# Half routers over more places, three of them in the next round, and pool's late operations behind its wait for an odd place

## What is computed

```python
x = x + conv(ln_c(x))            # ln_c(x) * sigmoid(conv3x3([max_c, mean_c]))
t = to_tokens(x)                 # (16, 112*112, 64)
n = ln_t(t)
probs = softmax(n @ router_w + router_b)
top_p, top_i = top_k(probs, 2);  top_p = top_p / sum(top_p)
t = t + sum_k top_p[k] * (n @ expert_w[top_i[k]] + expert_b[top_i[k]])
```

## Time and profile before

| | |
|---|---|
| median of 3 runs | 1394.77 us (1394.36 to 1395.02) |
| profiled execution, its own time | 1395.69 us |
| its span, first to last instruction | 1393.8 us |
| PE busy | 1294.6 us, 93% |
| DVE busy | 1240.0 us, 89% |
| POOL busy | 1066.0 us, 76% |
| ACT busy | 1052.0 us, 75% |

### The profile page before, as it was taken

How to read it: one execution, slowest core, us unless ns; L and a number is a source line. 1 busy time by engine, 2 the same in 40 slices (tenths; PEclk the granted TensorE clock), 3 DMA queues, 4 the chain that set the end, 5 groups by cost and what they waited for, 6 DMA issues and landing times.

```text
span 1393.8 us, 33104 instructions
## 1 busy us (share of the span) xinstructions
PE 1294.6 (93%) x11750; PEld 612.6 (44%) x11750; DVE 1240.0 (89%) x1527; ACT 1052.0 (75%) x3950; POOL 1066.0 (76%) x643
## 2 busy tenths in 40 slices
PE   8964999999999999999999999999999898889998
PEld 8853444444444444444444444444444332333332
DVE  6787799988999899998999799998999879998887
ACT  5677898888998889888898889888898533444442
POOL 5333787887888787877878878878878878789885
PEclk9955999999999999999999999999999999999999
DMA  6443466676666666576666666676666555657774
GB/s 224 120 123 89 132 207 206 174 224 199 198 187 213 194 204 199 173 226 199 199 200 199 199 200 200 187 217 192 207 203 175 163 166 162 175 167 205 205 204 144
DMA packets 85845, 259.97 MB, mean 187 GB/s; under 512 B 13744, under 2 KB 13744, under 8 KB 85680
## 3 DMA queue, kind: packets, MB, share of 16 engines
q1 hardware_dynamic: 85680, 257.85, 62.0%
HBM read 206.42 MB, written 51.38 MB: 185 GB/s over the span
## 4 chain that ended last, share of the span: by engine, by line
PE 56%; DVE 23%; issue 9%; POOL 2%; ACT 2%; DVEq 0%; POOLq 0%; ACTq 0%
PE moe L568 34%; DVE gx L714 13%; PE tm L493 8%; PE gb L514 8%; PE tm L507 2%; DVE ge L736 2%; DVE stats L691 2%; PE moe L562 2%; PE tm L553 2%; DVE ot L727 1%; DVE oh L749 1%; PE tm L592 1%; DVE u L799 1%; POOL dl L1265 1%; ACT sq L965 1%
## 5 line engine op out<-in xcount | busy, mean ns | idle before, releaser
L568 PE MATMUL moe<-gx,wc 128*64 128x448 f32 x3584 | 803.5, 551 | 0.0
L714 DVE TENSOR_TENSOR gx<-gb,xd 128x896 f32<-128x896 f32 x672 | 710.7, 1086 | 77.3 <-PE gb L514 72.9
L1205 POOL TENSOR_TENSOR gx<-gs,xd 128x896 f32<-128x896 f32 x224 | 492.8, 2200 | 228.0 <-ACT gs L1003 158.7
L965 ACT ACTIVATE sq<-xct 112x64 f32<-112x64 f32 x1400 | 338.4, 246 | 7.5 <-DVE early_s L701 2.1
L1003 ACT ACTIVATE gs<-gb 128x896 f32<-128x896 f32 x224 | 205.3, 916 | 176.4 <-PE gb L514 170.9
L568 PEld LDWEIGHTS moe<-gx,wc 128*64 128x64 f32 x3584 | 219.9, 136 | 201.6 <-issue 159.2
L965 ACT ACTIVATION_READ_ACCUMULATOR sq<-xct 112x1 f32 x1400 | 265.5, 190 | 0.0
L1222 POOL TENSOR_TENSOR tt<-xc,a1s 128x896 f32<-128x896 f32 x112 | 235.1, 2099 | 11.3 <-issue 9.7
L514 PE MATMUL gb<-s,cg 32*128 32x448 f16 x1792 | 175.6, 358 | 53.2 <-DVE gx L714 51.8
L514 PEld LDWEIGHTS gb<-s,cg 32*128 32x128 f16 x1792 | 48.0, 91 | 383.2 <-DVE gx L714 348.7
L493 PE MATMUL tm<-rhs,xa 64*112 64x74 f32 x2800 | 184.6, 272 | 10.6 <-ACT early_l L950 5.2
(11 more groups left out here) (94 smaller groups left out, 1090.0 us busy)
## 6 DMA issues: line engine op xcount, KB each, us to landing
xd<-in_x_dram SPq DMA_DIRECT2D x448, 224.0 KB, 4.0
xa<-in_x_dram SPq DMA_DIRECT2D x112, 448.0 KB, 4.5
xc<-in_x_dram SPq DMA_DIRECT2D x112, 448.0 KB, 4.8
out_dram<-ot SPq DMA_DIRECT2D x112, 448.0 KB, 3.6
gx<-in_const_g_dram SPq DMA_DIRECT2D x1, 384.0 KB, 5.5
cf<-in_const_f_dram SPq DMA_DIRECT2D x1, 333.5 KB, 3.1
cf<-in_L_ffn_expert_b_dram SPq DMA_DIRECT2D x12, 1.0 KB
gx<-in_L_ffn_expert_w_dram SPq DMA_DIRECT2D x1, 128.0 KB, 5.3
```

Source lines behind the costliest of these rows:

```text
L568: last = pe.matmul(moe[b * CH:(b + 1) * CH, c, 0:HALF], wc[:, k * CH:(k + 1) * CH], gx[:, u, b, :], start=False, stop=(k == KT - 1), skip_ ...
L714: dve.tensor_tensor(gx[:, i, :, :], gb[:, 2 * slot:2 * slot + 2, 0:HALF], xd[:, v % 2, :, c * HALF:(c + 1) * HALF], ALU.mult).then_inc(sca ...
L965: last = act.activation(sq[:, n, :], xct[:, step % 2, n, :], ACT.Square, accum_out=to[:, 1, lo + n:lo + n + 1])
L1205: pool.tensor_tensor(gx[:, ND + j, :, :], gs[:, j, :, :], xd[:, v % 2, :, j * HALF:(j + 1) * HALF], ALU.mult).then_inc(scaled_p, 1)
```

## The change

The half routers get other places. Half 0 has ten, 12 to 21: top; ge; key and key_max; oh1; dl; top2 and d; ge2; key2; key_max2; oh2. Half 1 has the first six of them at 22 to 27, and its last four operations go to three places of the next round: ge2 to place 0, key2 and key_max2 to place 4, oh2 to place 5. They count on a semaphore of their own, b_late, as B_LATE, and B_DVE has four operations less. ScalarE's part moves with them: `gates` of half 0 from step 8 to 9, the second widening of half 0 from 9 to 10, the first of half 1 from 11 to 12, `gates` of half 1 from 12 to step 0 of the next round, its second widening from 13 to step 2 of the next round. On pool the second, summed and scaled gates of half 0 move from steps 10, 11, 12 to 11, 12, 13; of half 1 first_gates moves from step 13 to step 0 of the next round, second_gates to step 2, summed and scaled gates to step 4, and all of these stand behind `router` and behind the wait for the odd place. The waits of pool for places are 1, 2, 3, 6, 7, 8 and 9 in rounds before 8 (26 is gone); in round 8 also 12 to 27, and in rounds 8 and 9 the late places 0, 4 and 5. rho has two buffers, since pool scales with the old one in step 4, after the next one has been written.

```diff
+B_LATE = ("ge2_1", "key2_1", "key_max2_1", "oh2_1")
 B_DVE = (tuple(n + "1" for n in ROOT) + ("r1", "av", "part_sum", "v2")
          + tuple(n + "2" for n in ROOT) + ("r2", "rho") + tuple(n + "_0" for n in HALF_ROUTER)
-         + tuple(n + "_1" for n in HALF_ROUTER))
+         + tuple(n + "_1" for n in HALF_ROUTER if n + "_1" not in B_LATE))
 B_POOL = ("lg_0", "bias_0", "lg_1", "bias_1", "m1_0", "m2_0", "qb_0", "qg_0", "m1_1", "m2_1", "qb_1",
           "qg_1")
 B_NORM = ("e1", "pool_max", "pool_mean", "am", "e2")
-B_ACT = ("sig", "wide_0", "g1_0", "g2_0", "qa_0", "wide2_0", "wide_1", "g1_1", "g2_1", "wide2_1", "qa_1")
+B_ACT = ("sig", "wide_0", "qa_0", "g1_0", "g2_0", "wide2_0", "wide_1", "g1_1", "g2_1", "qa_1", "wide2_1")
...
+        rhos = sb("rhos", [W, 2, 2 * H])
...
-        PLACE_END = {1: "t_a1", 2: "y_a1", 3: "r1", 6: "v2", 7: "t_a2", 8: "y_a2", 9: "rho",
-                     26: "key_max2_1"}
-
-        TAIL_END = {1: "t_a1", 2: "y_a1", 3: "r1", 6: "v2", 7: "t_a2", 8: "y_a2", 9: "rho"}
-        HALF_END = ("top", "ge", "key_max", "dl", "d", "ge2", "key_max2", "oh2")
-        for place in range(16):
-            TAIL_END[12 + place] = f"{HALF_END[place % 8]}_{place // 8}"
+        ROOT_END = {1: "t_a1", 2: "y_a1", 3: "r1", 6: "v2", 7: "t_a2", 8: "y_a2", 9: "rho"}
+        HALF_END = {12: "top_0", 13: "ge_0", 14: "key_max_0", 15: "oh1_0", 16: "dl_0", 17: "d_0", 18: "ge2_0",
+                    19: "key2_0", 20: "key_max2_0", 21: "oh2_0", 22: "top_1", 23: "ge_1", 24: "key_max_1",
+                    25: "oh1_1", 26: "dl_1", 27: "d_1"}
+        LATE_END = {0: "ge2_1", 4: "key_max2_1", 5: "oh2_1"}
 
         def vector_place(eng, r, place):
 
-            ends = TAIL_END if r == PAIRS else PLACE_END
-            if 1 <= r <= PAIRS and place in ends:
-                b_done(eng, r, B_DVE, ends[place])
+            if r <= PAIRS and place in ROOT_END:
+                b_done(eng, r, B_DVE, ROOT_END[place])
+            if r == PAIRS and place in HALF_END:
+                b_done(eng, r, B_DVE, HALF_END[place])
+            if PAIRS <= r <= PAIRS + 1 and place in LATE_END:
+                b_done(eng, r - 1, B_LATE, LATE_END[place])
...
                     own(r, f"top_{h}")
                     at_top(lg, top, rows).then_inc(b_dve, 1)
                 elif place == 2:
-                    largest_key(r, h, "", rows)
+                    tie_key(r, h, rows)
+                    first_of_ties(r, h, rows)
                 elif place == 3:
-                    first_expert(r, h)
+                    first_expert(r, h, rows)
                 elif place == 4:
-                    second_logit(r, h)
+                    logits_left(r, h, rows)
                 elif place == 5:
-                    own(r, f"top2_{h}")
-                    at_top(dl, top2, rows).then_inc(b_dve, 1)
+                    second_logit(r, h, rows)
                 elif place == 6:
-                    largest_key(r, h, "2", rows)
+                    second_at_top(r, h, rows, B_DVE)
+                elif place == 7:
+                    second_tie_key(r, h, rows, B_DVE)
+                elif place == 8:
+                    second_of_ties(r, h, rows, B_DVE)
                 else:
-                    second_expert(r, h)
+                    second_expert(r, h, rows, B_DVE)
+
+            def late_router(r, place):
+
+                if place == 0:
+                    second_at_top(r, 1, second, B_LATE)
+                elif place == 4:
+                    second_tie_key(r, 1, second, B_LATE)
+                    second_of_ties(r, 1, second, B_LATE)
+                elif place == 5:
+                    second_expert(r, 1, second, B_LATE)
...
-                if due(count := b_at(r, len(B_POOL), 0)):
+                if due(count := b_at(r - 1, len(B_POOL), 0)):
...
                     scale(r)
-                elif 12 <= place < 20:
+                elif 12 <= place < 22:
                     half_router(r, 0, place - 12)
-                elif place >= 20:
-                    half_router(r, 1, place - 20)
+                elif place >= 22:
+                    half_router(r, 1, place - 22)
...
+                    if tail:
+                        late_router(r - 1, 2 * step)
                     if Bp:
                         gate(r, step, False)
...
+                    if tail:
+                        late_router(r - 1, 2 * step + 1)
                     if Bp:
                         gate(r, step, True)
...
-                elif step == 8:
+                elif step == 9:
                     gates(r, 0)
-                elif step == 9:
+                elif step == 10:
                     widen(r, 0, "2")
-                elif step == 11:
+                elif step == 12:
                     widen(r, 1, "")
-                elif step == 12:
+
+            def late_router(r, step):
+
+                if step == 0:
                     gates(r, 1)
-                elif step == 13:
+                elif step == 2:
                     widen(r, 1, "2")
...
+                    if tail:
+                        late_router(r - 1, step)
                     if Bp:
                         router(r, step)
...
-                elif step == 10:
+                elif step == 11:
                     second_gates(r, 0)
-                elif step == 11:
+                elif step == 12:
                     summed_gates(r, 0)
-                elif step == 12:
+                elif step == 13:
                     scaled_gates(r, 0)
-                elif step == 13:
+
+            def router_tail(r, step):
+
+                if step == 0:
                     first_gates(r, 1)
-
-            def router_tail(r, step):
-
-                if step == 0:
+                elif step == 2:
                     second_gates(r, 1)
-                elif step == 1:
+                elif step == 4:
                     summed_gates(r, 1)
-                elif step == 2:
                     scaled_gates(r, 1)
...
-                    if tail:
-                        router_tail(r - 1, step)
                     if Bp:
                         router(r, step)
                     if ahead:
                         vector_place(pool, r, 2 * step + 1)
+                    if tail:
+                        router_tail(r - 1, step)
+                    if ahead:
                         scale_unit(r, v + 1, 0)
```

## The result

| | before | after |
|---|---|---|
| median, same chip | 1394.57 us | 1415.87 us (1415.30 to 1417.47) |
| ratio, 95% interval | 1 | 1.0149 [1.0136, 1.0162] |
| span of the profiled execution | 1393.8 us | 1414.0 us |
| mean granted clock of TensorE | 0.974 | 0.960 |

What follows compares the result with a forecast made beforehand. PE's own work sets a 10.92 us floor per step; the excess is PE stalled behind VectorE. Terms of -14.7 us from the profiled 1395.69 gave 1381, and the median, 0.9 lower, 1380 us; range 1365 to 1396.

Steps and rivals of the forecast that it cites:

- The floor and the places: PE's own work sets 10.92 us a step; a VectorE place holds about 1.4 us free, and more stalls PE.
- Step 12: Takes the even pair key and key_max, and oh1: about 11.25 us, unchanged within 0.1.
- step 2: Steady rounds: key2 and key_max2 at its even place cost +0.33 us; oh2 at its odd place is free.
- Step 1: Steady rounds: loses a 0.78 us stall from pool's late sum, gains a 0.8 stall at L807, so comes out even.
- L794's wait of 1.18 us: Step 0: the root's wait for e behind pool's late dl goes; the step falls to 10.92 us, -0.97.
- Step 4's lag: Pool's gx comes 3.9 us late, costs TensorE nothing in step 5, and is worked off by step 8.
- the term of +1.5 us for steps 6 to 8: Late pool work lengthens key of step 7 and dl of step 8: +1.5 us a round, bounds 0 and +3.
- The rule of the tie: A waiting VectorE operation gets in before pool's next one if that has a wait of its own in front.
- Rival 3: Pool always goes first, decided at ge of step 6 against parts; slower, 1403 us (1398 to 1406), chance 0.18.
- Rounds 1 and 8: Round 1 gives away four operations, -2 us (-4 to 0); round 8, without first pass, -2 (-6 to +4).
- Round 9 and what follows: Round 9 receives the four operations that round 1 gives away: +0.5 us, bounds 0 and +2.
- 8.0 + 3.2: Forecast gains: steps 6 to 13 save 8.0 us over six rounds, steps 0 to 2 save 3.2 over five.

Runs made afterwards that it cites:

- the kernel with a small tail: Changed kernel with pool's summed and scaled gates of half 1 in step 4 cut to 8 of 112 rows in rounds 3 to 9: 1375.68 us.
- the one wait added: Changed kernel with pool also waiting for oh1 (place 15) before its gx of step 7 in rounds 2 to 7: 1378.05 us, ratio 0.9874.
- the later pause: Changed kernel with pool waiting for its own gx before tt at step 7's odd place in rounds 2 to 7: 1397.50 us, ratio 1.0015.

## Why the prediction was wrong, point by point

- *The floor and the places: right.* Steps 9, 10, 11, 13 and 0 came to 10.92, 10.92, 11.11, 10.92 and 10.92 (forecast 10.92, 10.92, 11.17, 10.92, 10.92). Step 12 is 11.23 (11.25), step 2 costs 0.38 more (0.33). Step 1 is even, 11.73. L794's wait of 1.18 us is gone, and L842, the same operation as L807, takes 1.83 (forecast 2 with a stall of 0.8; measured 0.80):

```profile
783.89 0.27 DVE L829 TENSOR_SCALAR p<-e 112x224 int32<-112x224 int32 x1
...
789.36 1.83 DVE L842 SCALAR_TENSOR_TENSOR u<-u 112x224 f32<-112x224 f32 x1
```

- *Step 4's lag: right in size and in how fast it is worked off, wrong in what it meets.* gx there starts 3.9 us after rho, and step 5 still takes 10.92, as forecast:

```profile
666.88 2.10 POOL L1318 TENSOR_TENSOR q<-lg,dl 112x896 f32<-112x896 f32 x1 [2.70 <-DVE rhos L874]
669.05 1.75 POOL L1324 TENSOR_TENSOR q<-q,rhos 112x896 f32<-112x896 f32 x1
670.77 2.10 POOL L1249 TENSOR_TENSOR gx<-gs,xd 128x896 f32<-128x896 f32 x1
```

The sum counted 1.2 us of idle time in step 5 and 0.5 in step 6, which leaves 2.2 at the start of step 7. Measured, pool's idle time in the two steps is used up (busy 10.84 of 10.92 and 11.23 of 11.23 us), and the bias of step 7, 4.54 us into its step before (690.80 after 686.26), is 6.13 us into it now (699.03 after 692.90): 1.6 us late. So the lag wasn't worked off too slowly. But 1.6 us is more than the pause of 0.65 us between bias and gx in which oh1 had got in, and the idle time that the prediction set against the lag was made of just such pauses. In the kernel before, all twelve of oh1 in the steady rounds (both halves) had one of 0.65 to 0.67 us behind the operation that they waited for.
- *The failed step: the term of +1.5 us for steps 6 to 8, with bounds 0 and 3.* Against steps 6, 7 and 8 as the places alone would make them, the lag cost 8.0 us in this round (11.23 + 19.21 + 11.14, less the forecast's 11.39 + 11.25 + 10.92). Over the six rounds it is 46.1 us where 9 stood, 37 more; the forecast missed by 36. Three things were left out of it. It priced key of step 7 and dl of step 8, and not oh1 at place 15, which stands between them and beside pool's bias; key lost 0.3 and dl nothing. Its upper bound let pool pass once; with the pause gone, oh1 was passed twice after its first wait. And it had no price for the clock after a stall of 5 us.
- *The rule of the tie: falls.* The prediction took a wait of its own in front of pool's operation as the sign that VectorE gets in. Both gx and tt have one and passed oh1; and in the kernel with a small tail, ge got in before the very lg, without a wait, that passes it in the earlier trace rows. The page "SBUF — State Buffer" of the Trainium skill, section "Who interferes with whom", says that who issues first gets the pair for the whole instruction. That the other waits for the whole of it, the trace bears out. The prediction took it to mean as well that a VectorE operation that waits is always next, and that the trace doesn't bear out: oh1 starts 1.8 us before gx.
- *Rival 3: the right sign by the wrong place.* It stood at 1403 with 0.18, and was to decide at ge of step 6 against parts. There VectorE won (ge 1.73 us, parts stretched to 1.89), and key2 of step 2 won too (0.71). Pool doesn't always go first, so the rival falls as it was told; the mechanism that it had is the one that decided, 13 us larger.
- *Rounds 1 and 8:* -6.1 up to the start of round 2 (forecast -2; 1.9 of it lies ahead of round 1's gates) and -2.1 (forecast -2). Round 9 and what follows: +1.4 (+0.5).

So the gain that was forecast is there, and the pass took it back. With the one wait added, rounds 2 to 7, cut as above, gain 11.3 us, and the sum had about 11.2 for them (8.0 + 3.2). That the whole kernel then comes to 1378 us, near the 1380, is in part luck: what lies before round 2 gained 4 us more than forecast in the changed kernel.

## What to carry to other kernels

Where operations of GpSimd hold up those of VectorE, as here, lag put on GpSimd is not free until it is worked off. Idle time that absorbs the lag is also the pause in which VectorE gets in. So follow GpSimd's queue operation by operation to the first real pause, and price every two-input VectorE operation on the way at all that may pass it, not only at what is running. A wait that gives GpSimd a pause just there can be worth more than the work it delays. And a bound for a stall of TensorE that may reach some microseconds needs a term for the clock that follows.

## What the runs showed of the hardware that was not expected

A boundary here is an end of a GpSimd operation at which a VectorE operation was waiting and another GpSimd operation followed. Counted over the timelines of all twelve kernels:

```text
pause between the two, 0.01 to 0.78 us       VectorE got in at 127 of 127
no pause, next is gx                         VectorE got in at   0 of  18
no pause, next is tt                                            46 of  69
no pause, next is lg                                             4 of   6
no pause, next is parts                                         36 of  37
no pause, next is pooled, the bias or a sum                     66 of  66
```

- At every pause counted VectorE got in; 0.08 us was enough 19 times, 0.01 us once. Pool waited there for ScalarE (107 times) or for its own last operation (19 times), never for the operation that got in.
- Eleven of the 23 that did not get in before tt, and the one before parts, started at most 0.06 us before the end of the running operation, when the next one had started too or was about to; of the other twelve, nine are oh1, passed for the second time.
- Without a pause the outcome goes with the operation that follows; that is a count, not a test. Why gx always passes and pooled never does stays open: neither a wait in front of it, nor how long VectorE has waited (ge got in after 1.56 us, oh1 didn't after 1.86 and 3.90), nor how far the running operation is (key lost 0.43 us into tt, ge won 0.40 us into parts) sorts the cases. No run was made that varies the operation alone.
- TensorE's granted clock fell to 0.50 at every one of the six stalls of 5 us in the changed kernel, and after four of the six stalls of 2.95 us with the later pause, one like the other; what tells those apart isn't seen in these rows.
